# Second GCN pass with node steps between the quarters of the sums, and eight turns per loop in both softmax layers

## The chip, the cores and the metric

The kernel runs on one core of one Trainium2 chip. The time is device microseconds of one execution, from its start to its end. Before the change it is 5070.54 us, the median of 3 runs (5068.86 to 5072.62). TensorE is PE in the rows (its weight loads PEld), VectorE is DVE, ScalarE is ACT, GpSimd is POOL, and SyncE, which issues plain DMAs here, is SP.

## The reference

6250 nodes with 256 features each, and 106250 edges sorted by destination. Two graph blocks follow each other. What is computed, cut to what matters:

```python
h = relu(layernorm(x))
# block 1: two GCN layers and a projection
for W, b, g, c in ((W6, b6, ln6_g, ln6_b), (W7, b7, ln7_g, ln7_b)):
    t = layernorm(h) * g + c
    msg = (t @ W.T)[row] * (dis[row] * edge_weight * dis[col])[:, None]    # and a loop at each node
    h = h + relu(segment_sum(msg, col) + b)
x = x + h @ Wp.T + bp
h = relu(layernorm(x))
# block 2: a GAT layer with 4 heads (segment softmax of leaky_relu(a_src + a_dst), weighted segment sum),
x1 = prelu(gat(h))
# then a transformer layer (segment softmax of q[dst] . k[src] / 16, weighted segment sum of v[src])
out = prelu(segment_sum(v[src] * alpha) + x1 @ Wskip + bskip)
return x + out
```

## The kernel before, in words

Everything is fp32. The edges are cut into 52 groups of 2048 (`NGW`), each of 16 columns of 128 edges (`UW`). A column of 128 edges is one gather: POOL issues one indirect DMA that fetches 128 rows of 1 KB or a little more from a table in HBM, by source node, into `G` (`L558` in the GCN layers, `L859` in the GAT layer, `L1520` in the transformer layer). `G` has four buffers of 16 columns each, so POOL runs up to four groups ahead. Since the edges are sorted, a group's destinations lie in a window of 128 nodes. DVE makes a one-hot matrix `oh` per column (edge by node of the window), times the edge's weight in the GCN layers. PE multiplies `oh` with the gathered rows and adds up 16 columns in PSUM (`ps`). ACT evicts the sums to `stage`. Rows of a node that two groups share are carried over by a small matmul with `scol`. A loop over further windows (`nwin`) exists for sparse places; with these inputs there is one window per group, so a turn of a loop is one group.

Four layers run one after the other, with a barrier of all engines between them: `gcn_layer` with `layer == 1`, `gcn_layer` with `layer == 2`, `softmax_layer` with `gat=True`, `transformer_layer`. Each layer has one program per engine. The programs wait for each other by semaphores alone, and each engine works in its written order.

In the GCN layers, the sums of window w-1 are worked up to node rows while window w's turn runs. This is `node` on DVE and ACT, and `step(n, j)` on PE. In layer 1 PE has two steps: transposing `a` (sums plus the node's own row), and the product with the layer's weights (`psO`). In layer 2 it has six, in a chain with DVE and ACT between:

- step 0, `turn`: transpose `a`; ACT evicts it to `lt` (`L743`). Step 1, `multiply`: `psO`. DVE adds bias, relu and residual, which gives `o1` (`L626`, `L632`).
- step 2: transpose `o1`, ACT `lt`. Step 3: `psP`, the projection. DVE makes `o2`, its statistics (`L635`, `L637`, `L639`) and `nb`, the normalised row (`L651`); ACT takes the root (`L751`), DVE the inverse `rd` (`L654`).
- step 4: transpose `nb`, ACT `lt`. Step 5: `psG`, the GAT table's row. ACT scales and evicts it to `t3` (`L758`), and signals `s_res`.

SP then stores `o2` and `t3` (`L580`, `L581`). DVE's `node` of the next window waits before it writes `o1` (`s_st`) until those stores have landed. The three quarters of four one-hots each that a window needs first (`spread`, q = 0 to 2, `L612`) are made at the start of DVE's turn, so behind DVE's whole `node` of the window before and ahead of the next `a`; the last quarter is made inside `node`. PE adds a quarter of the sums when its gathers (`s_g`) and its one-hots (`s_oh`) are there, and signals it (`s_ohu`).

PE's program of the GCN layers is a loop over 13 times four groups. The softmax layers are written by `passes`: `body` once or three times by hand ahead, then a loop whose body holds `NBW` = 4 groups one behind another, then the rest by hand. There are 12 rounds of that loop in each of the two layers, on PE, DVE, ACT and SP. POOL has no loop: its gathers are written out. In a `body` of DVE there are two branches that jump over code for further windows (`logits_more`, `aggregate_more`; in the transformer layer `L1642` and `L1662`); PE, ACT and SP have such branches too. They are taken in every turn here.

Of the kernel before, what the change touches and what calls it, by code (L numbers as in the profile page):

```python
# [36 lines left out]
AGW = 264  # L37
UW = 16
GW = UW * P
NGW = NC // UW  # L40
NBW = 4
QW = 4
LN_EPS = 1e-5
BIG = 1.0e30
IOA = bass.IndirectOffsetOnAxis
# [474 lines left out]
def gcn_layer(nc, m, tag, layer):  # L520
# [7 lines left out]
    with ExitStack() as c:  # L528
# [151 lines left out]
        def _(pe):  # L680
# [25 lines left out]
                    if j == 5:  # L706
                        multiply(n, 2, psG, m.gw, AGW, s_lt3, s_prod3)

            steps = 2 if layer == 1 else 6

            pe.sem_inc(s_ohu, UW)
            with pe.Fori(0, NGW // NBW) as t:
                for b in range(NBW):
                    nwin, past = load_pack(nc, m, pe, t * NBW + b)
                    base = past + (t * NBW + b)
                    with pe.Fori(0, nwin) as i:
                        w = base + i
                        for j in range(steps):
                            step(w, j)
                        pe.wait_ge(s_ev, w + 1)  # L720
                        hold(m, pe)
                        for u in range(UW):
                            if u == UW - 1:
                                pe.wait_ge(s_scol, w + 1)
                                nc.tensor.matmul(ps[0:1, 0:D], scol[:], stage[:], start=False, stop=False)
                            if u % QW == 0:
                                pe.wait_ge(s_g[b][u // QW], t * (16 * QW) + 16 * QW)
                                pe.wait_ge(s_oh, w * UW + u + QW)
                            last = nc.tensor.matmul(ps[:, 0:D], oh[:, u, :], G[:, b, u, :], start=(u == 0), stop=(u == UW - 1))  # L729
                            if u % QW == QW - 1 and u < UW - 1:  # L730
                                last.then_inc(s_ohu, QW)
                        last.then_inc(s_ohu, QW)
            base, = load_wide(nc, m, pe, NGW, ("base",))
            for j in range(steps):
                step(base, j)

        @block.scalar
        def _(act):
# [6 lines left out]
            def node(n):  # L745
# [5 lines left out]
                nc.scalar.activation(sd[:], mv[:, 1:2], ACT.Sqrt, bias=m.eps[:, 0:1]).then_inc(s_dev, 1)  # L751
                if layer == 2:
                    evict(n, 2, s_turn3, s_lt3)
                    act.wait_ge(s_rd, n + 1)
                    act.wait_ge(s_st, n * ST + ST)
                    act.wait_ge(s_prod3, n + 1)
                    hold(m, act)
                    nc.scalar.activation(t3[:], psG[:, 0:AGW], ACT.Copy, scale=rd[:, 0:1]).then_inc(s_res, 1)  # L758

            act.wait_ge(s_zero, 1)  # L760
            act.sem_inc(s_ev, 1)
            with act.Fori(0, NGW) as k:
                nwin, past = load_pack(nc, m, act, k)
                base = past + k
                with act.Fori(0, nwin) as i:
# [2 lines left out]
                    act.wait_ge(s_ohu, (w + 2) * UW)  # L768
                    hold(m, act)
                    nc.scalar.activation(stage[:], ps[:, 0:D], ACT.Copy).then_inc(s_ev, 1)  # L770
                act.sem_inc(s_done, 1)
            base, = load_wide(nc, m, act, NGW, ("base",))
            node(base)


def softmax_layer(nc, m, tag, gat):
# [11 lines left out]
    with ExitStack() as c:  # L788
# [48 lines left out]
        def passes(eng, body):  # L837

            body(0, 0, 0, 0, agg=False)
            with eng.Fori(0, (NGW - 1) // NBW) as t:  # L840
                for j in range(1, NBW + 1):
                    body(t * NBW + j, t + j // NBW, t * 2 + j // 2, j % NBW)
            for k in range((NGW - 1) // NBW * NBW + 1, NGW):
                body(k, k // NBW, k // 2, k % NBW, lead=k < NGW - 1)
            body(NGW, NGW // NBW, NGW // 2, NGW % NBW, logits=False, lead=False)

# [609 lines left out]
def transformer_layer(nc, m):  # L1456
# [4 lines left out]
    with ExitStack() as c:  # L1461
# [29 lines left out]
        def passes(eng, body):  # L1491

            for k in range(3):
                body(k, k // NBW, k // 2, k % NBW)
            with eng.Fori(0, (NGW - 4) // NBW) as t:
                for j in range(3, 3 + NBW):
                    body(t * NBW + j, t + j // NBW, t * 2 + j // 2, j % NBW)
            for k in range((NGW - 4) // NBW * NBW + 3, NGW + 2):
                body(k, k // NBW, k // 2, k % NBW)

        def parts(k):
# [610 lines left out]
```

## Time and profile before

| | |
|---|---|
| median of 3 runs | 5070.54 us |
| profiled execution | 5070.05 us, its span from first to last instruction 5068.3 us |
| busy: PE, DVE, ACT, POOL | 3792.3 (75%), 2616.1 (52%), 873.7 (17%), 3225.0 (64%) us |
| TensorE clock granted, mean | 0.817 |
| first GCN layer, second | from about 165 us, from about 1235 us |
| GAT layer, transformer layer | from about 2414 us, from about 3745 us |
| gathers | 3328, 955 to 963 ns of POOL each |

The busy share of an engine is an average over four layers that have different limits. Which one sets the pace is read layer by layer: from the distance between one eviction of the sums and the next (a group), and from what each engine waits for in between. A POOL row shows the writing of a gather's descriptors; about 0.30 us lies between two of them even when nothing holds POOL up. fp32 matmuls of 256 columns stand as two records each, in PE's rows.

### The profile page before, as it was taken

To read this page: it belongs to the slowest core of one execution; us is meant where nothing else is said; L and a number is where in the kernel's file an instruction comes from. 1 tells how busy PE (TensorE), PEld (TensorE's weight loads), DVE (VectorE), ACT (ScalarE), POOL (GpSimd) and SP (SyncE) were. 2 spreads that over 40 slices of the span, in tenths; PEclk is the share of its full clock that TensorE was granted. 3 is DMA by queue.
4 is the path that set the end of the run, shared out by engine and by line. 5 is a ranking of instruction groups with operands and counts; after the bars stand their busy time and mean duration, and the time that the engine had idled before them with its cause. 6 is when DMAs were issued, how large, how long until landed. Compare 5 with 4: busy or idle time off the path is not lost. (4 is left out here: it accounts for less than half of the span.)

```text
span 5068.3 us, 77690 instructions
## 1 busy us (share of the span) xinstructions
PE 3792.3 (75%) x16038; PEld 2830.3 (56%) x16039; DVE 2616.1 (52%) x9965; ACT 873.7 (17%) x2343; POOL 3225.0 (64%) x3401
## 2 busy tenths in 40 slices
PE   2466666666767767767688888887869888888898
PEld 2244444443444544444566666666746666666666
DVE  8544444443333333333566666666745555555554
ACT  4100000000111111111111111111113333333333
POOL 3577777776777776662776666666437665566662
PEclk7778777777777777777788888878879999999999
DMA  5544444444444444442444444444224443344332
GB/s 158 139 129 131 130 131 129 129 133 115 135 133 132 135 132 123 124 126 63 115 125 113 107 109 104 105 106 108 79 67 129 118 112 105 104 110 109 107 107 57
DMA packets 323559, 585.83 MB, mean 116 GB/s; under 512 B 82891, under 2 KB 216070, under 8 KB 322950
## 3 DMA queue, kind: packets, MB, share of 16 engines
q0 software_dynamic: 159744, 440.25, 32.3%
q1 hardware_dynamic: 144153, 125.73, 8.1%
q10 hardware_dynamic: 19056, 12.87, 0.9%
q8 instruction: 245, 4.01, 0.4%
q14 instruction: 361, 2.96, 0.2%
HBM read 514.81 MB, written 63.78 MB: 114 GB/s over the span
## 5 line engine op out<-in xcount | busy, mean ns | idle before, releaser
L558 POOL DMA_INDIRECT g_G<-t,srcI x1664 | 1589.9, 955 | 550.2 <-issue 500.5
L729 PE MATMUL g_ps<-g_G,g_oh 128*128 128x256 f32 x3328 | 981.9, 453 | 262.9 <-DMA g_G<-t,srcI 239.4
L1520 POOL DMA_INDIRECT g_G<-t,srcI x832 | 792.1, 952 | 452.0 <-PE g_ps L1862 232.3
L859 POOL DMA_INDIRECT g_G<-t,srcI x832 | 801.5, 963 | 416.6 <-issue 242.1
L729 PEld LDWEIGHTS g_ps<-g_G,g_oh 128*128 128x128 f32 x3328 | 751.6, 231 | 501.6 <-issue 260.5
L612 DVE TENSOR_SCALAR g_oh<-iota,g_relx,g_wx 128x128 f32<-128x128 f32 x1664 | 461.0, 361 | 333.4 <-PE g_ps L729 319.9
L1851 PE MATMUL g_psA<-g_win,g_ohT 128*128 128x257 f32 x1664 | 539.2, 408 | 108.9 <-issue 74.3
L1601 DVE CUSTOM_DVE_ANT_0 g_junk<-g_G,g_psA 128x257 f32<-128x257 f32 x832 | 350.9, 422 | 507.9 <-PE g_psA L1851 392.3
L1862 PE MATMUL g_ps<-g_G,g_oh 128*128 128x257 f32 x1664 | 515.0, 393 | 44.3 <-ACT g_stage L1970 44.3
L1258 PE MATMUL g_ps<-g_Gp,g_oh 128*128 128x264 f32 x1664 | 519.1, 473 | 0.0
L1258 PEld LDWEIGHTS g_ps<-g_Gp,g_oh 128*128 128x128 f32 x1664 | 385.1, 240 | 84.8
L1862 PEld LDWEIGHTS g_ps<-g_G,g_oh 128*128 128x128 f32 x1664 | 317.5, 195 | 127.0 <-ACT g_oh L1974 58.5
L1851 PEld LDWEIGHTS g_psA<-g_win,g_ohT 128*128 128x128 f32 x1664 | 285.2, 197 | 176.8 <-issue 107.0
L1239 PE MATMUL g_psA<-g_win,g_ohT 128*128 128x4 f32 x1664 | 290.3, 310 | 2.6 <-issue 2.4
L1239 PEld LDWEIGHTS g_psA<-g_win,g_ohT 128*128 128x128 f32 x1664 | 285.2, 270 | 4.5 <-issue 3.4
L619 DVE TENSOR_TENSOR g_a<-g_stage,g_own 128x256 f32<-128x256 f32 x106 | 45.3, 427 | 451.1 <-ACT g_stage L770 451.1
L1974 ACT ACTIVATE g_oh<-g_oh,g_p 128x128 f32<-128x128 f32 x832 | 253.4, 388 | 6.5
L1958 ACT ACTIVATE g_ohT<-g_psT 128x512 f32<-128x512 f32 x208 | 124.2, 597 | 751.4 <-PE g_psT L1811 751.4
L1589 DVE TENSOR_SCALAR g_oh<-iota,g_relx 128x128 f32<-128x128 f32 x832 | 246.3, 298 | 0.0
L1163 DVE TENSOR_TENSOR g_Gp<-g_G,g_psP 128x1024 f32<-128x1024 f32 x208 | 238.8, 1201 | 0.0
L770 ACT ACTIVATE g_stage<-g_ps 128x256 f32<-128x256 f32 x104 | 39.8, 383 | 1145.2 <-PE g_ps L729 1145.2
L952 DVE TENSOR_SCALAR g_oh<-iota,g_relx 128x128 f32<-128x128 f32 x832 | 180.6, 302 | 73.7 <-DVE g_run L1134 36.4
(289 smaller groups left out, 4250.0 us busy)
## 6 DMA issues: line engine op xcount, KB each, us to landing
g_G<-t,srcI POOLq DMA_INDIRECT x3328, 2.8
g_own<-t SPq DMA_DIRECT2D x159, 128.0 KB
t<-g_t SPq DMA_DIRECT2D x53, 132.0 KB
g_rec<-t SPq DMA_DIRECT2D x53, 132.0 KB
g_rec<-h SPq DMA_DIRECT2D x53, 128.5 KB
x<-g_o SPq DMA_DIRECT2D x53, 128.5 KB
g_rec<-x SPq DMA_DIRECT2D x53, 128.5 KB
t<-g_t4r SPq DMA_DIRECT2D x53, 128.5 KB
```

Source lines behind the costliest of these rows:

```text
L558: pool.indirect_dma_start(G[:, b, u, :], None, table, IOA(ap=m.srcI[:, g * UW + u:g * UW + u + 1], axis=0)).then_inc(s_g[b][u // QW], 16)
L612: nc.vector.tensor_scalar(oh[:, u, :], m.iota[:], relx[:, u:u + 1], wx[:, u:u + 1], ALU.is_equal, ALU.mult).then_inc(s_oh, 1)
L729: last = nc.tensor.matmul(ps[:, 0:D], oh[:, u, :], G[:, b, u, :], start=(u == 0), stop=(u == UW - 1))
L859: pool.indirect_dma_start(G[:, b, u, :], None, table, IOA(ap=m.srcI[:, g * UW + u:g * UW + u + 1], axis=0)).then_inc(s_g[b], 16)
L1239: last = nc.tensor.matmul(psA[:, u * H:u * H + H], ohT[:, u * P:u * P + P], win[:, b % 2, :], start=True, stop=True)
L1258: last = nc.tensor.matmul(ps[:, 0:RW_], lhs, rows_of(bp, u), start=(u == 0), stop=(u == UW - 1))
L1520: pool.indirect_dma_start(G[:, b, u, :], None, m.t4, IOA(ap=m.srcI[:, g * UW + u:g * UW + u + 1], axis=0)).then_inc(s_g[b][u // QW], 16)
L1589: return nc.vector.tensor_scalar(oh[:, b % 4, u, :], m.iota[:], relx[:, b % 2, u:u + 1], None, ALU.is_equal)
L1601: nc.vector.tensor_tensor_reduce(out=junk[:, u % 2, :], in0=G[:, b, u, :], in1=psA[:, u % 2, 0:RW], scale=1.0, scalar=0.0, op0=ALU.mult, o ...
L1851: nc.tensor.matmul(psA[:, u % 2, 0:RW], ohT[:, u, :], win[:, r, :], start=True, stop=True).then_inc(s_pa, 1)
L1862: last = nc.tensor.matmul(ps[:, 0:RW], oh[:, b2, u, :], G[:, b2, u, :], start=(u == 0), stop=(u == UW - 1))
L1974: last = nc.scalar.activation(src[:, u, :], src[:, u, :], ACT.Copy, scale=p[:, r, u:u + 1])
```

## The change

It has two parts.

In `gcn_layer`, PE's steps for the node rows are no longer all ahead of the window's sums. A table `between` says which steps stand ahead of which column. In layer 1 nothing moves. In layer 2 steps 0 and 1 stay ahead of column 0, step 2 stands ahead of column 4, step 3 ahead of column 8, step 4 ahead of column 12, and step 5 behind column 15 and its signal. On ACT, the scaled eviction of `psG` to `t3` is taken out of `node` into `result`, and stands behind the eviction of the window's sums instead of ahead of it. DVE, SP and POOL keep their programs in this layer.

In both softmax layers, `passes` puts 8 groups into the loop body in place of 4 (`NLOOP`). There are 6 rounds in place of 12, and the groups written out by hand ahead of and behind the loop are the same as before. The number of groups, what a group does and its order on each engine stay. The buffers stay `NBW` = 4.

```diff
--- before.py
+++ after.py
@@ -40,6 +40,7 @@
 NGW = NC // UW
 NBW = 4
 QW = 4
+NLOOP = 8
 LN_EPS = 1e-5
 BIG = 1.0e30
 IOA = bass.IndirectOffsetOnAxis
@@ -706,7 +707,8 @@
                     if j == 5:
                         multiply(n, 2, psG, m.gw, AGW, s_lt3, s_prod3)
 
-            steps = 2 if layer == 1 else 6
+            between = {0: (0, 1)} if layer == 1 else {0: (0, 1), 4: (2,), 8: (3,), 12: (4,)}
+            behind = () if layer == 1 else (5,)
 
             pe.sem_inc(s_ohu, UW)
             with pe.Fori(0, NGW // NBW) as t:
@@ -715,11 +717,12 @@
                     base = past + (t * NBW + b)
                     with pe.Fori(0, nwin) as i:
                         w = base + i
-                        for j in range(steps):
-                            step(w, j)
-                        pe.wait_ge(s_ev, w + 1)
-                        hold(m, pe)
                         for u in range(UW):
+                            for j in between.get(u, ()):
+                                step(w, j)
+                            if u == 0:
+                                pe.wait_ge(s_ev, w + 1)
+                                hold(m, pe)
                             if u == UW - 1:
                                 pe.wait_ge(s_scol, w + 1)
                                 nc.tensor.matmul(ps[0:1, 0:D], scol[:], stage[:], start=False, stop=False)
@@ -730,8 +733,10 @@
                             if u % QW == QW - 1 and u < UW - 1:
                                 last.then_inc(s_ohu, QW)
                         last.then_inc(s_ohu, QW)
+                        for j in behind:
+                            step(w, j)
             base, = load_wide(nc, m, pe, NGW, ("base",))
-            for j in range(steps):
+            for j in range(2 if layer == 1 else 6):
                 step(base, j)
 
         @block.scalar
@@ -751,11 +756,13 @@
                 nc.scalar.activation(sd[:], mv[:, 1:2], ACT.Sqrt, bias=m.eps[:, 0:1]).then_inc(s_dev, 1)
                 if layer == 2:
                     evict(n, 2, s_turn3, s_lt3)
-                    act.wait_ge(s_rd, n + 1)
-                    act.wait_ge(s_st, n * ST + ST)
-                    act.wait_ge(s_prod3, n + 1)
-                    hold(m, act)
-                    nc.scalar.activation(t3[:], psG[:, 0:AGW], ACT.Copy, scale=rd[:, 0:1]).then_inc(s_res, 1)
+
+            def result(n):
+                act.wait_ge(s_rd, n + 1)
+                act.wait_ge(s_st, n * ST + ST)
+                act.wait_ge(s_prod3, n + 1)
+                hold(m, act)
+                nc.scalar.activation(t3[:], psG[:, 0:AGW], ACT.Copy, scale=rd[:, 0:1]).then_inc(s_res, 1)
 
             act.wait_ge(s_zero, 1)
             act.sem_inc(s_ev, 1)
@@ -768,9 +775,13 @@
                     act.wait_ge(s_ohu, (w + 2) * UW)
                     hold(m, act)
                     nc.scalar.activation(stage[:], ps[:, 0:D], ACT.Copy).then_inc(s_ev, 1)
+                    if layer == 2:
+                        result(w)
                 act.sem_inc(s_done, 1)
             base, = load_wide(nc, m, act, NGW, ("base",))
             node(base)
+            if layer == 2:
+                result(base)
 
 
 def softmax_layer(nc, m, tag, gat):
@@ -837,10 +848,10 @@
         def passes(eng, body):
 
             body(0, 0, 0, 0, agg=False)
-            with eng.Fori(0, (NGW - 1) // NBW) as t:
-                for j in range(1, NBW + 1):
-                    body(t * NBW + j, t + j // NBW, t * 2 + j // 2, j % NBW)
-            for k in range((NGW - 1) // NBW * NBW + 1, NGW):
+            with eng.Fori(0, (NGW - 1) // NLOOP) as t:
+                for j in range(1, NLOOP + 1):
+                    body(t * NLOOP + j, t * (NLOOP // NBW) + j // NBW, t * (NLOOP // 2) + j // 2, j % NBW)
+            for k in range((NGW - 1) // NLOOP * NLOOP + 1, NGW):
                 body(k, k // NBW, k // 2, k % NBW, lead=k < NGW - 1)
             body(NGW, NGW // NBW, NGW // 2, NGW % NBW, logits=False, lead=False)
 
@@ -1492,10 +1503,10 @@
 
             for k in range(3):
                 body(k, k // NBW, k // 2, k % NBW)
-            with eng.Fori(0, (NGW - 4) // NBW) as t:
-                for j in range(3, 3 + NBW):
-                    body(t * NBW + j, t + j // NBW, t * 2 + j // 2, j % NBW)
-            for k in range((NGW - 4) // NBW * NBW + 3, NGW + 2):
+            with eng.Fori(0, (NGW - 4) // NLOOP) as t:
+                for j in range(3, 3 + NLOOP):
+                    body(t * NLOOP + j, t * (NLOOP // NBW) + j // NBW, t * (NLOOP // 2) + j // 2, j % NBW)
+            for k in range((NGW - 4) // NLOOP * NLOOP + 3, NGW + 2):
                 body(k, k // NBW, k // 2, k % NBW)
 
         def parts(k):
```

PE in the second layer, in one turn of its loop, from step 1 on. `g_psT` is a transpose, `g_psO`, `g_psP`, `g_psG` are the products of steps 1, 3 and 5, `g_ps` are the sums. Before:

```order
L691 MATMUL g_psO<-w,g_lt 128x256
L692 MATMUL g_psO<-w,g_lt 128x256
L685 MATMUL g_psT<-ident,g_o 128x128
L686 MATMUL g_psT<-ident,g_o 128x128
L691 MATMUL g_psP<-wp,g_lt 128x256
L692 MATMUL g_psP<-wp,g_lt 128x256
L685 MATMUL g_psT<-ident,g_nb 128x128
L686 MATMUL g_psT<-ident,g_nb 128x128
L691 MATMUL g_psG<-gw,g_lt 128x264
L692 MATMUL g_psG<-gw,g_lt 128x264
L727 ISA
L728 ISA
```

The rest of this turn is the sixteen products of the sums in a row, with the carry in front of the last. Now, from the same place:

```order
L692 MATMUL g_psO<-w,g_lt 128x256
L693 MATMUL g_psO<-w,g_lt 128x256
L730 ISA
L731 ISA
L732 MATMUL g_ps<-g_G,g_oh 128x256 x4
L686 MATMUL g_psT<-ident,g_o 128x128
L687 MATMUL g_psT<-ident,g_o 128x128
L731 REGISTER_ALU
L732 MATMUL g_ps<-g_G,g_oh 128x256 x4
L692 MATMUL g_psP<-wp,g_lt 128x256
L693 MATMUL g_psP<-wp,g_lt 128x256
L731 REGISTER_ALU
```

Between two quarters of the sums there is now one step. The end of the same turn on PE now:

```order
L732 MATMUL g_ps<-g_G,g_oh 128x256 x4
L686 MATMUL g_psT<-ident,g_nb 128x128
L687 MATMUL g_psT<-ident,g_nb 128x128
L731 REGISTER_ALU
L732 MATMUL g_ps<-g_G,g_oh 128x256 x3
L728 MATMUL g_ps<-g_stage,g_scol 1x256
L732 MATMUL g_ps<-g_G,g_oh 128x256
L692 MATMUL g_psG<-gw,g_lt 128x264
L693 MATMUL g_psG<-gw,g_lt 128x264
```

The product for `g_psG` has moved behind the last sum. ACT in the same layer before, one turn:

```order
L743 ACTIVATE g_lt<-g_psT 128x256 x2
L751 ACTIVATE g_sd<-g_mv,eps 128x1
L743 ACTIVATE g_lt<-g_psT 128x256
L755 ISA
L758 ACTIVATE g_t<-g_psG,g_rd 128x264
L768 ISA
L770 ACTIVATE g_stage<-g_ps 128x256
L765 REGISTER_ALU x2
```

And now (line numbers are 7 higher from here on):

```order
L748 ACTIVATE g_lt<-g_psT 128x256 x2
L756 ACTIVATE g_sd<-g_mv,eps 128x1
L748 ACTIVATE g_lt<-g_psT 128x256
L775 ISA
L777 ACTIVATE g_stage<-g_ps 128x256
L762 ISA
L765 ACTIVATE g_t<-g_psG,g_rd 128x264
L772 REGISTER_ALU x2
```

The eviction to `g_t` stands behind that of the sums, `g_stage`.

## Rows read from the trace of the kernel before

**Rows 1.** windows: start:end, length, busy (count) of PE, PEld, DVE, ACT, POOL, then clock, DMA.

```profile
165.00:1235.00 1070.00, 691.48 (x2086) 460.24 (x2086) 446.46 (x1571) 55.83 (x158) 793.83 (x833) 0.78 0.46 128
1235.00:2414.00 1179.00, 828.92 (x2722) 568.15 (x2722) 429.46 (x1465) 121.89 (x317) 796.67 (x833) 0.73 0.42 122
...
3745.00:5068.00 1323.00, 1159.33 (x5468) 884.92 (x5466) 713.79 (x3525) 430.88 (x1249) 789.02 (x829) 0.96 0.39 106
```

**Rows 2.** timeline of POOL: gathers of both GCN layers; start us, us, engine, line.

```profile
169.35 1.10 POOL L558 DMA_INDIRECT g_G<-t,srcI  x1 [0.53 <-issue]
...
1215.08 0.95 POOL L558 DMA_INDIRECT g_G<-t,srcI  x1 [0.30 <-issue]
...
1236.20 0.95 POOL L558 DMA_INDIRECT g_G<-t,srcI  x1 [0.38 <-issue]
...
1885.52 0.94 POOL L558 DMA_INDIRECT g_G<-t,srcI  x1 [1.45 <-ACTq L771]
...
2327.76 0.95 POOL L558 DMA_INDIRECT g_G<-t,srcI  x1 [0.30 <-issue]
```

**Rows 3.** timeline of ACT: evictions of the sums in the GCN layers.

```profile
1223.29 0.38 ACT L770 ACTIVATE g_stage<-g_ps 128x256 f32<-128x256 f32 x1 [14.69 <-PE g_ps L729]
...
1263.30 0.38 ACT L770 ACTIVATE g_stage<-g_ps 128x256 f32<-128x256 f32 x1 [8.15 <-PE g_ps L729]
...
2397.02 0.38 ACT L770 ACTIVATE g_stage<-g_ps 128x256 f32<-128x256 f32 x1 [7.66 <-PE g_ps L729]
```

**Rows 4.** timeline, all engines, one turn of the second layer.

```profile
1419.74 0.38 ACT L770 ACTIVATE g_stage<-g_ps 128x256 f32<-128x256 f32 x1 [8.71 <-PE g_ps L729]
...
1429.11 0.35 DVE L651 TENSOR_SCALAR g_nb<-g_o,g_mv 128x256 f32<-128x256 f32 x1
...
1431.31 0.23 DVE L663 TENSOR_SCALAR g_relx<-relW,steps 128x16 f32 x1 [0.32 <-DVE g_wx L662]
...
1432.82 7.19 PE L729 MATMUL g_ps<-g_G,g_oh 128*128 128x256 f32 x30
...
1434.54 0.35 SPq L581 DMA_DIRECT2D t<-g_t  x1
```

**Rows 5.** groups by line, second layer: two products of one shape.

```profile
L691 PE MATMUL g_psP<-wp,g_lt 128*128 128x256 f32 x102 | 60.8, 700 | 33.4 <-ACT g_lt L743 33.4
...
L691 PE MATMUL g_psO<-w,g_lt 128*128 128x256 f32 x104 | 34.8, 416 | 34.1 <-ACT g_lt L743 34.1
```

**Rows 6.** DMA issues on the page: the gathers, median us to landing.

```profile
g_G<-t,srcI POOLq DMA_INDIRECT x3328, 2.8
```

**Rows 7.** timeline of ACT: evictions of the sums in the GAT layer.

```profile
2568.79 0.39 ACT L1388 ACTIVATE g_stage<-g_ps 128x264 f32<-128x264 f32 x1
...
2639.49 0.39 ACT L1388 ACTIVATE g_stage<-g_ps 128x264 f32<-128x264 f32 x1
...
3558.25 0.39 ACT L1388 ACTIVATE g_stage<-g_ps 128x264 f32<-128x264 f32 x1
```

**Rows 8.** timeline of ACT: evictions of the sums in the transformer layer.

```profile
3932.05 0.36 ACT L1970 ACTIVATE g_stage<-g_ps 128x257 f32<-128x257 f32 x1
...
3977.59 0.37 ACT L1970 ACTIVATE g_stage<-g_ps 128x257 f32<-128x257 f32 x1
...
4935.77 0.37 ACT L1970 ACTIVATE g_stage<-g_ps 128x257 f32<-128x257 f32 x1
```

**Rows 9.** timeline, transformer layer: PE after the jump back, DVE before a fourth turn.

```profile
3906.90 1.22 PE L1851 MATMUL g_psA<-g_win,g_ohT 128*128 128x257 f32 x2 [6.04 <-issue]
...
3980.36 0.42 DVE L1601 CUSTOM_DVE_ANT_0 g_junk<-g_G,g_psA 128x257 f32<-128x257 f32 x1 [3.17 <-issue]
```

**Rows 10.** DMA queues that bring instructions: second GCN layer, then transformer layer.

```profile
q14 instruction: 7, 0.06, 0.0%
...
q8 instruction: 119, 1.95, 0.8%
q14 instruction: 198, 1.62, 0.4%
```

## The prediction

> **What bounds the kernel now.** I read the windows by layer first, then the timeline of POOL and the evictions of the sums, then one turn in full. The evictions of the sums give the pace of a layer, since one stands in every group.
>
> In the first GCN layer POOL never waits. Its gathers start every 1.2585 us: 831 intervals from 169.35 to 1215.08 are 1045.7 us [rows 2]. That is 20.1 us per group of 16. The last eviction of the sums stands at 1223.29, 8.2 us behind the last gather [rows 3]. So this layer is bound by POOL, and PE, 691 us busy in 1070 [rows 1], waits for it.
>
> In the second GCN layer the evictions run from 1263.30 to 2397.02, which are 51 turns of 22.23 us [rows 3]. POOL could do a turn in 20.1. It runs ahead until all four buffers are full, and from then on its first gather of a group waits for ACT's signal that a buffer is free, as at 1885.52 (1.45 us, "<-ACTq L771") [rows 2]. Its 831 intervals take 2327.76 - 1236.20 = 1091.6 us, and PE is still 69.3 us of work behind its last gather [rows 2, 3]. The bound is the chain of a turn: the sums of 16 columns are one block (7.2 us at the fast clock, from 1432.82), and ahead of it the steps of the node rows go to and fro between PE, DVE and ACT from 1419.74 on, 13.1 us in which PE mostly waits [rows 4].
>
> In the GAT and the transformer layer PE is the busiest engine (1159 of 1323 us in the transformer layer, clock 0.96) [rows 1]. Their turns are even but for one place. In the GAT layer three turns are 2639.49 - 2568.79 = 70.70 us, 23.57 each, while ten rounds of four turns are 3558.25 - 2568.79 = 989.46, 98.95 per round; the fourth turn, with the jump back, therefore takes 28.25, 4.7 us more than the others [rows 7]. In the transformer layer two turns are 45.54, 22.77 each; ten rounds are 4935.77 - 3932.05 = 1003.7, 100.4 each, which is 9.3 us more than four times 22.77 [rows 8]. Two stalls make this up. Behind the jump back PE has a gap of 6.04 us "<-issue", and before the round's last turn DVE has one of 3.17 us "<-issue", released by nothing but its own sequencer [rows 9]. The instruction queues show what the sequencers wait for: in the second GCN layer 7 packets of instructions come in, in the transformer layer 119 and 198 [rows 10]. So a loop body that long isn't kept, and is fetched anew in each round.
>
> **The second layer.** No instruction is added or removed. The question is what the pace becomes when steps 2 to 4 lie between quarters. I work out a turn's length from the turn shown. DVE is the ring to follow, since in its order the twelve one-hots of the next window stand between `nb` and the next `a`.
>
> From the eviction of the sums to the end of `nb` it is 1429.11 + 0.35 - 1419.74 = 9.7 us [rows 4]. Into this come a quarter of the sums between `psO` and the second transpose, and one between that transpose and `psP`. A quarter is 7.19 / 30 x 8 = 1.9 us at the fast clock. Both take the place of waits for DVE and ACT of 1.2 and 0.7 us, so they add 0.7 + 1.2. Step 5 now stands ahead of the next transpose of `a`; about 0.8 of its 1.2 us aren't hidden by the eviction and `a`. From the end of `nb` to the end of `relx` it is 1431.31 + 0.23 - 1429.46 = 2.1 us, and twelve one-hots are 3.4 (0.28 each). The sum is 9.7 + 1.9 + 0.8 + 2.1 + 3.4 = 17.9, less 0.4 since `a` stands behind the eviction: 17.5 us. PE's own chain ends sooner, near 15, because the quarters fill its waits.
>
> Two things make it longer. The first is the clock: `psO` runs mostly at the fast level (2.4 GHz), 416 ns a record, and `psP`, of the same shape, mostly at the slow one (1.2 GHz), 700 ns [rows 5]. With everything at the slow level the two quarters, `psP` and the other steps add 4 to 4.5 us, which gives 22. The second is the store. Before `o1` DVE waits until the stores of the node before have landed. Today the last is issued at 1434.54 [rows 4], long before. Now `psG` ends some 1 us behind the eviction of the sums, then come `t3` and the issue (2 us), and the landing, for which the nearest row is the gather's 2.8 us [rows 6]: about 6 us, where `o1` is wanted at 3.4. A quarter of the sums covers 1.9 of these 2.6, so it costs 0 to 1.5 us. The turn is thus 17.5 to 19 at the fast clock and 22 to 23 at the slow one, against 20.1 for POOL. In the first layer, where PE waits for gathers, the granted clock is 0.78, in the second 0.73 [rows 1]; at that mix a turn comes to about 19.8. I take the value below 20.1: the gathers set the pace. The closer PE gets to its limit the less it idles, and the clock was 0.96 where it was busy for 88% of the time [rows 1].
>
> The Trainium skill, in TensorE: Matmul & The Clock Gate, section "Loop structure matters more than you think", says that matmuls stay warm when they stand back to back and go cold when waits stand between them. By that rule a cut into quarters speaks against the change. What the slow level would give is the second case below, worked out from rows. The trace bears the rule out in part: PE is slow just after the long waits in a turn.
>
> Then the layer looks like the first one. The last gather comes 1091.6 - 1045.7 = 45.9 us sooner. The last eviction of the sums stands 8.2 us behind it in place of 69.3, 61.1 sooner. Behind it is the chain of the last node as before, with `psG` of the turn before ahead of its first transpose: 1 us, and 1 for a slower last quarter. Gain: 45.9 + 61.1 - 2 = 105 us.
>
> **The loops.** There are 6 rounds in place of 12 in both layers. A round's end costs 4.7 us in the GAT layer. In the transformer layer the 9.3 divide into about 2.4 for DVE's late start (3.17 less what stands there in other turns) and 6.9 for the jump back, PE's 6.04 with some slower matmuls behind it. Six fewer jumps back give 6 x 4.7 + 6 x 6.9 = 28 + 41 = 69 us. What is late next is nothing new: POOL needs 20.1 per group and these turns take 22.8 and 23.6. DVE's late start is at a branch over code that isn't run. Whether a round of eight turns has none, one, two or four of these isn't in the trace; by place it depends on how the code lies in the pieces that are fetched. Bounds: 12 x 2.4 = 29 us gained or 29 lost. I take two per round, as many as now, and 0.
>
> One price is unseen. ACT's and SP's bodies are short enough now that they show no gap at the jump. With twice the length they may be fetched too. ACT idles for several us in each turn, so I take 0. If it weren't hidden it would be at most a gap like PE's, 6 x 6 us per layer, less than the jump it goes with.
>
> The Trainium skill, in Runtime: NRT & Kernel Launch, section "Instruction fetch mechanics", says that instructions come in blocks of 16 KiB, two of which are held (more on TensorE), and that a taken branch to a block not held stalls. By that, each jump back stalls once whatever the body's length beyond that, as in the sum above. The packets of q8 are 1.95 MB / 119 = 16.4 KB each here, those of q14 8.2 KB [rows 10]. The same sentence would let forward branches stall too, which is the fifth case below.
>
> Sum: 5070 - 105 - 69 = 4896. The profiled execution is 5070.05 and the median 5070.54, so the same holds for the median.
>
> **The rivals.**
> 1. The gathers set the pace of layer 2, and half the jumps back go: 4896. For it: the turn above, and a first layer that already runs so. 62%.
> 2. The chain of a turn stays the bound in layer 2: clock at the slow level or the wait for the stores. At 21 us a turn the last eviction stands at 1263.30 + 51 x 21 = 2334, 63 us sooner than now. With the loops: 5070 - 63 - 69 = 4938. For it: 17.5 to 23 includes 20.1. Against it: a PE that is never idle. 17%.
> 3. Layer 2 as forecast, and fewer forward stalls in the long bodies: down to 4896 - 29 = 4867. 9%. Or stalls that the shorter loop didn't have eat half of the 69: 4931. 7%.
> 4. The long body doesn't help: the cost goes with the amount fetched and not with the jump. Then only layer 2 gains: 5070 - 105 = 4965. 2%.
> 5. Slower than before: forward branches stall in nearly every turn, since more engines (ACT and SP too) fetch through one queue and their pieces come late. The place is the two branches per body on DVE, or the windows that SP loads. The price is about 3 us in each of some 96 turns, 288 us, against 174 gained: 5184. It decides from 58 such stalls on. Against it: one stall in four turns now, in one of two layers. 2%.
> The last 1% is that nothing changes.
>
> The range that leaves out 2 in 10 at most reaches from the third case to the second with some more: 4862 to 4950. A measurement can tell 0.2%, 10 us, from no change. Faster: cases 1 to 4 and almost all else, 0.97. Within: 0.01. Slower: 0.02.
>
> **What would show it.** In the profile after: evictions of the sums in layer 2 every 20.1 us; POOL's gathers from its first to its last in about 1046 us with no wait for ACT; DMA (the gathers) as what PE waits for most in that layer; the GAT layer's first gather near 2310 in place of 2416. In both softmax layers, a long turn only at each eighth, 28 and 29 us, five times per layer and not eleven. Fewer packets of instructions wouldn't show it right or wrong; the gaps do. It is wrong if the turn in layer 2 is above 20.5, if POOL still waits for ACT there, or if gaps "<-issue" show on PE or DVE at new places within a round.

## Result, and the profile after

The changed kernel takes 4996.65 us (median of 4 runs, 4993.8 to 5010.87), the kernel before beside it 5071.58 (5068.86 to 5073.89, 4 runs). The ratio is 0.9857, 95% interval 0.9843 to 0.9871. It is faster by 75 us; 174 were forecast, and the time lies above the range of 4862 to 4950.

The windows by layer of the changed kernel, cut at the first gather of a layer; columns as in [rows 1]:

```profile
1239.06:2309.81 1070.75, 720.44 (x2722) 500.74 (x2722) 418.88 (x1465) 121.93 (x317) 792.86 (x837) 0.90 0.47 135
2309.81:3614.09 1304.28, 1070.30 (x5312) 878.70 (x5312) 889.67 (x3035) 196.35 (x472) 803.30 (x836) 0.81 0.41 105
3614.09:4993.10 1379.01, 1193.20 (x5477) 915.55 (x5477) 719.45 (x3543) 432.02 (x1250) 791.72 (x832) 0.93 0.38 102
```

Cut in the same way, the kernel before has:

```profile
2415.93:3741.03 1325.10, 1074.36 (x5312) 883.93 (x5312) 888.37 (x3035) 196.18 (x472) 802.06 (x835) 0.81 0.40 103
3741.03:5068.30 1327.27, 1161.89 (x5477) 887.03 (x5477) 717.44 (x3543) 431.84 (x1250) 792.07 (x832) 0.96 0.39 106
```

The second GCN layer went from 1179.7 us (2415.93 less 1236.20) to 1070.7, the GAT layer from 1325.1 to 1304.3, and the transformer layer from 1327.3 to 1379.0. So the first two gained 109 and 21 us, and the third lost 52.

POOL in the second GCN layer, its first and last gather, and the first of the GAT layer, answering to [rows 2]:

```profile
1239.06 0.95 POOL L559 DMA_INDIRECT g_G<-t,srcI  x1 [0.39 <-issue]
...
2283.31 0.94 POOL L559 DMA_INDIRECT g_G<-t,srcI  x1 [0.30 <-issue]
...
2309.81 0.95 POOL L870 DMA_INDIRECT g_G<-t,srcI  x1 [0.16 <-issue]
```

The 831 intervals take 1044.3 us: POOL doesn't wait for ACT any more. ACT's evictions of the sums there, answering to [rows 3]:

```profile
1264.40 0.38 ACT L777 ACTIVATE g_stage<-g_ps 128x256 f32<-128x256 f32 x1 [5.98 <-PE g_ps L732]
...
2290.60 0.38 ACT L777 ACTIVATE g_stage<-g_ps 128x256 f32<-128x256 f32 x1 [6.69 <-PE g_ps L732]
```

These are 51 turns of 20.12 us, and the last one stands 7.3 us behind the last gather, where it was 69.3.

The loss is in the transformer layer. The view of one line, here PE's second branch at the end of a turn, gives the length of its records (shortest/median/longest, in ns). Before, over the layer:

```profile
L1931 PEldq COMPARE_BRANCH  x52: 218/400/1302, 3806.1 to 5049.6; - x52
```

After, over the layer, then of turns one to four and five to eight of the loop's second round:

```profile
L1942 PEldq COMPARE_BRANCH  x52: 208/282/4678, 3679.2 to 4975.3; - x52
...
L1942 PEldq COMPARE_BRANCH  x4: 3862/3954/4142, 3909.9 to 3992.2; - x4
...
L1942 PEldq COMPARE_BRANCH  x4: 208/208/214, 4019.5 to 4093.7; - x4
```

An undisturbed jump takes 0.21 us. In half of the turns of the loop it takes about 4, and PE's timeline has the gap just behind it, at the start of the next turn:

```profile
3911.34 0.70 PE L1873 MATMUL g_ps<-g_G,g_oh 128*128 128x257 f32 x2
3915.84 0.79 PE L1862 MATMUL g_psA<-g_win,g_ohT 128*128 128x257 f32 x1 [3.80 <-issue]
```

The turns are long where the branch is. ACT's evictions of the sums, answering to [rows 8]:

```profile
3941.04 0.37 ACT L1981 ACTIVATE g_stage<-g_ps 128x257 f32<-128x257 f32 x1
3968.42 0.36 ACT L1981 ACTIVATE g_stage<-g_ps 128x257 f32<-128x257 f32 x1
...
4047.87 0.37 ACT L1981 ACTIVATE g_stage<-g_ps 128x257 f32<-128x257 f32 x1
4070.56 0.36 ACT L1981 ACTIVATE g_stage<-g_ps 128x257 f32<-128x257 f32 x1
```

A turn with the stall is 27.4 us, one without it 22.7 as before. The branch is at 3909.95, and PE works on until 3912.04: it still has matmuls queued, which cover the first 2 us. The turn gets 4.7 us longer all the same. Over the layer there are 25 of these stalls, counted as below, 99.3 us in all, mean 3.97. Before, there are 25 too, but they are 22.2 us, mean 0.89.

### The profile page after: what moved, and what is told of

Same layout as the page of the kernel before. It is cut to its first block and busy times, and to the rows that moved or that the text cites. A ratio compares the mean times of both kernels' runs of the same rounds, so it can differ in the third digit from the quotient of the medians.

```text
span 4993.1 us, 77288 instructions
## 1 busy us (share of the span) xinstructions
PE 3712.0 (74%) x16038; PEld 2788.4 (56%) x16039; DVE 2608.0 (52%) x9965; ACT 874.1 (18%) x2343; POOL 3223.4 (65%) x3401
## 5 line engine op out<-in xcount | busy, mean ns | idle before, releaser
L732 PE MATMUL g_ps<-g_G,g_oh 128*128 128x256 f32 x3328 | 1031.1, 460 | 479.6 <-DMA g_G<-t,srcI 379.5
L1862 PE MATMUL g_psA<-g_win,g_ohT 128*128 128x257 f32 x1664 | 562.4, 422 | 164.2 <-issue 138.9
L1873 PE MATMUL g_ps<-g_G,g_oh 128*128 128x257 f32 x1664 | 533.0, 405 | 11.1 <-ACT g_stage L1981 11.1
```

Of the source, the lines that this page charges most:

```text
L1862: nc.tensor.matmul(psA[:, u % 2, 0:RW], ohT[:, u, :], win[:, r, :], start=True, stop=True).then_inc(s_pa, 1)
L1873: last = nc.tensor.matmul(ps[:, 0:RW], oh[:, b2, u, :], G[:, b2, u, :], start=(u == 0), stop=(u == UW - 1))
```

## The experiments

**What is counted.** A "stall" is a record of that branch in the transformer layer behind which PE's sequencer starts its next one more than 0.6 us after the branch's own start; its length is that time, which is the record's duration and 0.06 us. "Landing" is where the branch's target stands. I counted it in the compiled programs: a turn is some 504 instructions of PE, and the packets of instructions for PE are 16,384 bytes; there are two per turn. 256 instructions of 64 bytes fill one packet (a "piece"), and taking the pieces to begin at multiples of 256 from the start of PE's program, a landing is a number from 0 to 255. From turn to turn of the loop it falls by about 8, since a turn is some 8 short of two pieces. The GAT layer stands ahead in the same program, so its longer loop moves the transformer's code by 186. In the changed kernel the eight landings are 219, 216, 207, 199, 190, 182, 173, 165: the first four stall. The starts of the packets for PE, read beside its branches in the changed kernel:

```
turn one: L1942 at 3909.95, 3.99 us; packets start at 3911.12 and 3915.01
turn six: L1942 at 4044.31, 0.21 us; packets start at 4045.56 and 4053.84
```

In both a packet starts some 1.2 us behind the branch, but only in turn one does PE wait for it. Turn five, landing at 190, has no long branch, but PE's sequencer stops within a few instructions behind it, at about 192: for 2.3 us in this round, for 2.0 to 3.0 us in all six. That is no stall by the count above. My theory: a landing in the last quarter of a piece (192 and up) that PE has only just entered needs the next piece, whose fetch has only just begun. The rival: a body of eight turns stalls because it is long.

The Trainium skill, in Runtime: NRT & Kernel Launch, section "Instruction fetch mechanics", gives blocks of 256 instructions, prefetched in sequence, and says that a taken branch whose target isn't in the two current ones stalls. The piece's size agrees with the 16,384 bytes here. The rule doesn't tell which jumps stall here, since all of these land at most one piece ahead.

Four kernels ran together first; the kernel before took 5068.81 us beside them.

*The second GCN layer alone.* Both softmax loops at four turns:

```diff
-NLOOP = 8
+NLG, NLT = 4, 4        # GAT, transformer
```

> The second GCN layer as changed, both softmax loops at four turns as before. Placement theory (PE stalls where its second branch at a turn's end lands in the last quarter of a 256-instruction fetch piece that it has only just entered; the two branches of the transformer layer then cost 3.9 us a turn): PE's program stands here as before, so 5071 - 106 = 4965 us, transformer layer 1327 us long. Length theory (a body of eight turns makes PE stall, wherever it stands): 4965 too. Third theory (the new second GCN layer slows later layers, by clock or queues): the transformer layer is some tens of us longer than 1327 here too, 4990 to 5010.

Measured: 4965.43 us, ratio 0.9794 (0.9778 to 0.9811). Transformer layer 1326.1 us, 24 stalls of 22.0 us in all. The GCN part is as forecast and does nothing to later layers. The third theory is out.

*Eight turns in the GAT layer only.*

```diff
-NLOOP = 8
+NLG, NLT = 8, 4
```

> As changed, but eight turns only in the GAT layer's loop, four in the transformer's. Length theory: the transformer layer is as before (1327 us), so 4965 - 21 (what the GAT loop gave) = 4944 us. Placement theory: the longer GAT program moves the transformer loop by 186 instructions in its fetch pieces, the second branch's targets stand at 219, 216, 207, 199 of 256 in all twelve rounds, so about 50 stalls of 3.9 us on L1942 in place of some 20 us: transformer layer about 1500 us, total about 5120 us, slower than the kernel before.

Measured: 5068.12 us, ratio 0.9996 (0.9987 to 1.0006). The transformer loop, the same four turns as in the run above, takes 1449.5 us in place of 1326.1:

```profile
L1942 PEldq COMPARE_BRANCH  x52: 211/3705/4447, 3679.5 to 5043.4; - x52
```

There are 49 stalls, 174.2 us in all. This ends the length theory: the loop isn't longer, it has only moved, and the whole gain of the GCN part is gone. My figure of 5120 was too high by 50: in every second round turns one and three stalled for 2.1 to 3.0 us only, and the layer got 123 us longer where the stalls grew by 152.

*Eight turns in the transformer layer only.*

```diff
-NLOOP = 8
+NLG, NLT = 4, 8
```

> As changed, but eight turns only in the transformer's loop, four in the GAT layer's. Length theory: transformer layer 1379 us as in the changed kernel, total 4965 + 52 = 5017 us. Placement theory: the first five turns of the loop stand as before (targets 33 to 4 of 256), only turns six to eight (252, 243, 235) in the last quarter: some 15 stalls of 3.9 us against six back edges saved at 6.9 us, transformer layer about 1340 us, total about 4980 us.

Measured: 4933.57 us, ratio 0.9728 (0.9712 to 0.9744). Transformer layer 1298.9 us, 30 stalls of 53.8 us. The eight turns cost nothing by themselves. Placement had 4980, 46 us too much, and the stalls stand elsewhere than it said. In turns six to eight, landings 252 to 235, 8 of 18 branches take over 2 us; the others 0.4 to 1.2. And turn five, which lands at 4 and so outside the last quarter, stalls in all six rounds, for 0.9 to 3.6 us. Its record in the first round:

```profile
L1942 PEldq COMPARE_BRANCH  x1: 3122/3122/3122, 3814.4 to 3814.4; - x1
```

So the last quarter is too narrow a rule: a landing just behind a piece's start stalls as well. The kernel before, with landings of 33 to 13 and stalls of 0.6 to 1.4 us, says the same.

*Never executed instructions on PE.* Ahead of PE's turns of the transformer layer, in the changed kernel (the branch is never entered):

```diff
                 turn_hot(0, 0, q)
+            nwin0, _ = load_pack(nc, m, pe, 0)
+            with pe.If(nwin0 > 1):
+                for _ in range(183):
+                    hold(m, pe)
             passes(pe, body)
```

> The changed kernel with 183 instructions that are never executed (a branch jumps over them) in PE's program ahead of the transformer layer's turns. All turns of the loop then have the second branch's target at 150 down to 96 of 256. Placement theory: the stalls on L1942 (25, 97.8 us) and the start of turn five go, transformer layer about 1280 us, total 4885 to 4900 us. Length theory, or queues or SP's longer program: the stalls stay, total 4997 us as the changed kernel.

Measured: 4903.97 us, ratio 0.9669 (0.9653 to 0.9685). All stalls are gone, and the layer with them gets 95.6 us shorter:

```profile
L1942 PEldq COMPARE_BRANCH  x52: 213/213/353, 3685.7 to 4885.7; - x52
```

```profile
3620.32:4903.70 1283.38, 1147.23 (x5477) 877.85 (x5477) 721.08 (x3543) 432.22 (x1250) 793.96 (x832) 0.97 0.40 110
```

The next four ran beside a kernel before of 5073.82 us.

*The same padding, one whole piece.* `range(252)`.

> The same padding as in the run with 183, but with 252 never executed instructions, which with the branch around them is 256, one whole fetch piece: the transformer loop stands in its pieces as in the changed kernel (targets 219 to 165). Placement theory: the 25 stalls of 3.9 us on L1942 come back, total 4997 us. If the branch or the padding itself had helped, by a pause or otherwise: 4904 us as with 183.

Measured: 4995.98 us, ratio 0.986 (0.9838 to 0.9883), 25 stalls of 98.7 us. It isn't the padding, it is the place.

*Every landing in the last quarter.* `range(27)`.

> Padding of 27: all eight turns of the loop have the target of L1942 at 250 down to 196 of 256. Placement theory, dose: 40 turns of the loop and some 5 ahead of it stall for 3.9 us, 45 x 3.9 = 175 us more than with padding 183: about 5080 us, slower than the kernel before, with the same instructions executed as in the runs with 183 and 252. Without placement: between 4904 and 4997.

Measured: 4990.7 us, ratio 0.9845 (0.9828 to 0.9861). The number of stalls was right, 45, and their length wrong: 129.2 us in all, mean 2.87. With landings from 230 to 250 the branch takes from 0.3 to 4.2 us, with 196 to 221 from 0.7 to 4.5, and the pattern comes back each third round. And the layer, 1365.1 us, isn't longer than with 25 stalls of 4 us (1371.2). The time is a clear miss by 90 us: a landing in that stretch doesn't say how long a stall is.

*One jump in place of two.* On PE:

```diff
+                with ExitStack() as more:
+                    if logits and agg:
+                        more.enter_context(pe.If(nwin + nwin2 > 2))
...                        # both branches of before, inside
```

> The changed kernel, with one outer branch on PE around the two at a turn's end, so that a turn ends in one jump over both pieces of unexecuted code in place of two jumps; its target stands at 223 to 196 of 256 in turns one to six, 189 and 183 in seven and eight. If a landing in the last quarter of a piece just entered is what stalls, the stalls stay, on the new line, in six turns of eight: about 5010 to 5030 us. If two jumps in quick succession are what stalls, they go: about 4900 us.

Measured: 5001.99 us, ratio 0.9858 (0.9842 to 0.9875), 8 us below the 5010 to 5030 that was expected if the stalls stay. The stalls are on the outer branch, L1921, in exactly the six turns with landings of 196 and up, and never in the two with 189 and 183. Two branches in a row aren't needed:

```profile
L1921 PEldq COMPARE_BRANCH  x50: 344/3642/4671, 3679.7 to 4961.6; - x50
```

*Sixteen turns, well placed.* `NLOOP = 16`, and padding with `range(102)`.

> Sixteen turns per loop in both softmax layers, with padding of 102 on PE so that the sixteen targets stand at 185 down to 63 of 256, none in the last quarter. Placement theory: no stall on L1942, three rounds' ends less in each layer, 3 x 4.4 + 3 x 6.9 = 34 us less than the run with 183: about 4870 us. Length theory: longer than that run, 4904 us or more.

Measured: 4865.2 us, ratio 0.9591 (0.9575 to 0.9607), no stall on L1942. GAT layer 1296.3 us, transformer layer 1258.5.

*Three kernels on another chip.* The eight runs above were on two chips; these, on a third: SP and ACT with short loops, all turns written out, and the kernel before with padding. Their edits are those of the last three runs below.

> As the run with padding 183, but SP and ACT keep loops of four turns, whose bodies stand in their stores (no gap at the jump back before the change); PE and DVE keep eight. If the new gaps at SP's and ACT's jump back (3.4 and 3.4 us, five times in a layer) are hidden: 4904 us as there. If they are on the path: up to 10 x 3.4 = 34 us less, 4870 us; and the GAT layer, 1307 us long there, would come to some 1298, the 7 us that my forecast for it missed.

> All 48 turns of the softmax loops written out, with never executed instructions inside PE's last branch so that each turn of the transformer layer is 512 of PE's instructions, two whole pieces: every target of L1942 stands at 123 of 256. Placement theory: no stall on L1942 in 48 turns, and against the sixteen-turn run (4865 us) two more jumps back go in each layer, 2 x (4.4 + 6.9) = 23 us: 4842 us. Length theory (long straight code makes PE or DVE wait for fetches): 4865 us or more.

> The kernel before, unchanged but for padding of 121 never executed instructions ahead of PE's turns of the transformer layer, which moves the targets of its second branch from 33 to 13 of 256 to 158 to 138. Placement theory: its 25 stalls (22 us in all) go too, 5071 - 22 = about 5050 us. Otherwise 5071.

Measured: 6158.86, 6114.28 and 6168.4 us beside a kernel before of 6156.4; ratios 0.9995 (0.9969 to 1.0022), 0.9931 (0.9898 to 0.9964), 0.9997 (0.9971 to 1.0024). Here is the GAT layer of the third, whose program there is that of the kernel before, without its ends:

```profile
2771.00:4600.00 1829.00, 1251.31 (x5249) 1005.26 (x5247) 864.58 (x2976) 194.35 (x464) 798.00 (x830) 0.67 0.27 74
```

POOL's own work is the same, but DMA moves 74 GB/s where [rows 1] and the windows above have over 100, the clock is 0.67, and DVE now waits for gathers that have been issued but not landed:

```profile
DVE g_oh L952 <- DMA g_G<-t,srcI: 354.7, 46, 10.4
```

What slowed the transfers wasn't looked into. The loops still gain there: against that kernel, the one with SP and ACT short has a GAT layer shorter by 31 us and a transformer layer shorter by 46. What eats this is the second GCN layer. As changed, and as before:

```profile
1436.18:2823.37 1387.19, 844.71 (x2722) 595.15 (x2722) 419.78 (x1465) 116.74 (x317) 791.78 (x837) 0.73 0.36 104
...
1436.87:2768.36 1331.49, 851.41 (x2722) 579.19 (x2722) 420.92 (x1465) 121.94 (x317) 823.89 (x836) 0.70 0.37 108
```

It is 56 us longer with the change, and 60 us longer in the kernel with all turns written out. A turn takes 25.1 us in place of 24.0, and in both POOL waits for ACT to free a buffer (276.6 and 180.1 us in all between 1460 and 2700). So POOL's work is not the bound there, before or after, and the new order makes a turn longer. Which wait does it wasn't tested. These times answer none of the three questions, so the kernels ran once more on a chip of the earlier runs, beside the one with padding 183 and a kernel before of 5071.36 us.

> The changed kernel with PE's padding of 183 once more, to stand beside the next run on one chip: 4904 us as before, no stall on L1942, GAT layer 1304 to 1307 us, transformer layer 1283 us.

Measured: 4902.45 us, ratio 0.967 (0.9654 to 0.9687); GAT 1304.8 us, transformer 1283.3.

*SP and ACT keep loops of four turns.* The loop's length depends on the engine:

```diff
         def passes(eng, body):
+            NLOOP = NBW if eng in SHORT else 2 * NBW      # SHORT: SP and ACT
```

> Padding 183 with SP and ACT in loops of four turns, PE and DVE in loops of eight. If the gaps at SP's and ACT's jump back are hidden: the same time as the run beside it, 4904 us, and the GAT layer 1304 to 1307. If they are on the path: up to 10 x 3.4 = 34 us less, and the GAT layer some 1298.

Measured: 4895.86 us, ratio 0.9656 (0.964 to 0.9672), its interval overlapping that of the run beside it. The gaps of SP and ACT at the jump back are gone (they were 3.4 to 3.6 us, five per layer and engine; ACT had none in the transformer layer). The GAT layer is 1304.9 us, unchanged: they were hidden there. The transformer layer is 1278.9, 4.4 us less, so SP's may cost a little.

*All 48 turns written out.* `NLOOP = 48`, padding with `range(130)`, and 26 more never executed `hold` in PE's last branch, so that a turn is 512 instructions and every landing 123:

```diff
                         pe.wait_ge(s_agx, xb2 + nwin2)
-                        hold(m, pe)
+                        for _ in range(27):
+                            hold(m, pe)
```

> All 48 turns written out in both softmax layers, each turn of the transformer layer 512 instructions of PE, targets of L1942 at 123 of 256. Placement theory: no stall on L1942, 4865 (sixteen turns) less 2 x (4.4 + 6.9) = 4842 us. If long straight code has a cost of its own: 4865 us or more.

Measured: 4842.66 us, ratio 0.9548 (0.9532 to 0.9564), the fastest of all. No jump back is left, and no stall on L1942:

```profile
L1942 PEldq COMPARE_BRANCH  x52: 213/213/343, 3663.2 to 4825.0; - x52
```

```profile
3598.06:4842.50 1244.44, 1128.74 (x5477) 869.08 (x5477) 717.18 (x3543) 431.84 (x1250) 791.59 (x832) 0.99 0.42 113
```

Long straight code has no visible price here: the forecast was 4842. The Trainium skill, in the section named above, names such stalls as one reason why kernels prefer full unrolling; this run agrees, with its landings placed. Written out without placing them wasn't run.

*The kernel before with padding 121.*

> The kernel before with padding of 121 on PE ahead of the transformer layer's turns, targets of the second branch at 158 to 138. Placement theory: its 25 short stalls, 22 us in all, go: about 5050 us. Otherwise 5071 us.

Measured: 5067.32 us, ratio 0.9992 (0.9982 to 1.0001): no difference that can be told. The forecast of about 5050 was missed. All 25 stalls went, and the transformer layer went from 1327.3 to 1317.6 us, 10 of the 22 us that they summed to. The rest must have been covered by PE's queued matmuls.

| kernel | landings in the loop | stalls, us in all | transformer layer | median |
|---|---|---|---|---|
| before | 33 to 13 | 25, 22.2 | 1327.3 | 5071.58 |
| changed | 219 to 165 | 25, 99.3 | 1379.0 | 4996.65 |
| GAT 8, transformer 4 | 219 to 199 | 49, 174.2 | 1449.5 | 5068.12 |
| GAT 4, transformer 8 | 33 to 4, 252 to 235 | 30, 53.8 | 1298.9 | 4933.57 |
| padding 183 | 150 to 96 | 0 | 1283.4 | 4903.97 |
| padding 252 | 219 to 165 | 25, 98.7 | 1371.2 | 4995.98 |
| padding 27 | 250 to 196 | 45, 129.2 | 1365.1 | 4990.7 |
| one jump | 223 to 183 | 37, 137.0 | 1386.6 | 5001.99 |
| sixteen turns | 185 to 63 | 0 | 1258.5 | 4865.2 |
| written out | 123 | 0 | 1244.5 | 4842.66 |

## Why the prediction was wrong, by its own steps

**The second layer: right.** Forecast 105 us; the kernel with this part alone is 5068.81 - 4965.43 = 103 us faster. The turn is 20.1 us, POOL's 831 intervals 1044.3 us (forecast 1046), the GAT layer's first gather at 2309.81 (2310). The fear of the slow clock went the other way: the layer's clock rose from 0.73 [rows 1] to 0.90. `psP`, 700 ns a record before [rows 5], is now

```profile
L692 PE MATMUL g_psP<-wp,g_lt 128*128 128x256 f32 x106 | 32.1, 385 | 0.7 <-ACT g_lt L748 0.7
```

The reason given for it, "the closer PE gets to its limit the less it idles", isn't borne out: PE is idle for 350 us of the layer now and for 351 before. What changed is where the idle time stands, no longer all ahead of one block; why that raises the clock wasn't tested. One term of the turn was too small. The wait for the stores was put at 0 to 1.5 us; DVE now waits for them 2.8 us in each of 53 turns:

```profile
L627 DVE SCALAR_TENSOR_TENSOR g_o<-g_psO,g_rec,rows 128x256 f32<-128x256 f32 x53 | 25.6, 484 | 151.1 <-DMA t<-g_t 148.8 <-issue 2.2
```

It didn't set the pace, since the turn is POOL's 20.1 us. That the new chain is shorter than the gathers is so on the chips of these runs only: on the one with slow transfers it isn't, and there the layer lost 56 to 60 us.

**The GAT loop: 28 forecast, 21 measured.** The jumps back went as said: eleven branches of 4.5 us on PE became five, and a long turn stands only at each eighth. Evictions of the sums, answering to [rows 7], 27.97 us for that turn and 23.66 for a usual one, and PE's gap there:

```profile
2529.45 0.39 ACT L1399 ACTIVATE g_stage<-g_ps 128x264 f32<-128x264 f32 x1
2557.42 0.39 ACT L1399 ACTIVATE g_stage<-g_ps 128x264 f32<-128x264 f32 x1
...
2628.26 0.39 ACT L1399 ACTIVATE g_stage<-g_ps 128x264 f32<-128x264 f32 x1
2651.92 0.39 ACT L1399 ACTIVATE g_stage<-g_ps 128x264 f32<-128x264 f32 x1
```

```profile
2537.25 0.56 PE L1310 MATMUL g_psR<-g_pf,ones 1*128 1x4 f32 x2 [5.13 <-issue]
```

In the profile the term is right: eleven long turns stood 49 us above the usual turn in all, five stand 22 above it, 27 less. The layer is only 21 shorter. Turns of 25.2 us stand among those of 23.7, with nothing in them but slower matmuls. The same turn of two rounds of the changed kernel (columns as in the windows):

```profile
2628.26:2651.96 23.70, 19.80 (x105) 16.14 (x104) 17.17 (x59) 3.77 (x11) 15.66 (x17) 0.86 0.45 111
2822.39:2847.60 25.21, 21.25 (x104) 17.12 (x103) 17.21 (x59) 3.68 (x10) 16.78 (x18) 0.80 0.42 110
```

The clock is 0.80 in place of 0.86, and the turn 1.5 us longer. There are five such turns in the loop's part and three before, some 3 us. But the kernel with the second layer alone, with its four turns per loop, has five too. And GAT layers of one and the same loop differ between profiles by as much as is missing: 1301.6 to 1308.5 us with eight turns, 1322.2 to 1329.1 with four. So the missing 7 us aren't explained. SP's or ACT's fetches are ruled out by the run with their loops short. Why the clock drops in those turns is open.

**The transformer loop: 41 forecast, a loss of 52 measured.** The term for the jumps back was near: with the stalls placed away the layer is 1283.4 us, 43.9 less than before. That this is so close to 41 is in part luck, since some 10 of it are the short stalls of the kernel before. Against that kernel with its stalls placed away (1317.6) it is 34.2, so 5.7 us for each jump back where 6.9 were forecast. The step that failed is "forward stalls: I take two per round, as many as now, and 0", with bounds of 29 us either way. I had priced only the branch stall that I had seen, DVE's of 2.4 us; that one indeed stayed the same (13 before, 13 after, mean 2.5 us in both). PE's own second branch had 25 stalls of 0.6 to 1.4 us before the change, and I never looked at its line. Queued matmuls cover about half of them, and they leave no long gap in PE's timeline; so they didn't show in the views of waits from which I took my rows. With the code moved by the GAT loop's growth there are 25 again, but 4 us long: 99.3 us of branches and 95.6 us of layer. The prediction says that "by place it depends on how the code lies in the pieces that are fetched", and rival 5 has forward branches that stall, but on DVE or SP, in nearly every turn, and for contention. The mechanism was the placement of PE's code, worth 96 us, and it belonged in the range.

**ACT's and SP's longer bodies: priced at 0, about right.** They are fetched now, as feared; 0 in the GAT layer, up to 4.4 us in the transformer layer.

**The signs I named.** "Gaps on PE at new places within a round" was the sign that it is wrong, and it is what shows.

The balance: 5070 - 106 - 21 + 52 = 4995, against 4996.65 measured; 106 is what the GAT layer's first gather came sooner, 2415.93 less 2309.81. With padding, 4903.97 is close to the 4896 forecast.

**What stays open.** The rule that tells a landing's stall. What the runs show is that landings from 63 to 189 were free in every run, that 196 to 223 took 2 to 4.7 us but for two of about 1 us with padding 27, that 230 to 252 and 4 took from 0.3 to 4.2 us, and 13 to 33 up to 1.4. Why the stalls change from round to round of one loop is open too; and DVE's stall of 2.5 us, which the kernels before and after both have. For DVE, whose packets have half the size, I found no placement rule that holds for all its turns.

## What to carry to other kernels

When code of a kernel grows or moves, loops behind it on the same engine move in the fetch pieces too, and their forward branches can change from free to several us per turn: compare the durations of every branch record before and after, also those hidden behind queued work. A few never executed instructions ahead of a loop are a test of one run, and here they gave 93 us. Where a loop has branches over rarely used code, place it so that they land in the middle of a piece, as in the runs with no stall. With a turn of a whole number of pieces, as in the one written out, one placement serves all turns.

An order that costs nothing while the gathers set the pace can cost where something else does, as in the second layer. It gave 103 us on one chip and took 56 to 60 on another.

## What the runs showed that I had not expected

- The same loop of four turns took 1326.1 or 1449.5 us, by nothing but the length of the layer ahead of it in PE's program.
- A forward branch that stalls costs up to 4.7 us on PE, its jump back 5.5 us in the transformer layer and 4.5 in the GAT layer.
- On the third chip, with the kernel before at 6156 us, a kernel worth 4.5% elsewhere gave 0.7%, and its second GCN layer was slower than before.
- Cutting the sums into quarters raised the granted clock of the layer from 0.73 to 0.90, with as much idle time on PE as before.
